# Two pairs of an attention round in one exp over four PSUM banks, the third in an exp of its own, and the vector work of the block moved to VectorE in parts behind the rounds

## What is computed

```
h = layernorm(x) * (1 + ca) + sa
q = h per head times Wq                      # 16 heads of 16 features
scores = q q^T * 4 ; attn = softmax(scores)  # 16 heads, 4096 x 4096
x = x + ga * ((attn q) Wp^T + bp)
h = layernorm(x) * (1 + cb) + sb
f = silu((layernorm(h) * gamma + beta) w1 + b1) w2 + b2     # 256 -> 1024 -> 256, weights dequantized from int32
x = x + gb * (h + 0.5 * f)
```

## Time and profile before

| | |
|---|---|
| median of 3 runs | 2073.87 us (2073.63 to 2074.2) |
| profiled execution, its time | 2074.52 us |
| its span in the trace | 2072.7 us |
| PE matmul busy | 1958.2 us, 94% of the span |
| ACT busy | 1966.9 us, 95% |
| DVE busy | 377.8 us, 18% |
| POOL busy | 70.4 us, 3% |

### The profile page before, as it was taken

The page is one execution under the profiler, slowest core; times in us unless marked ns, Lnnn a source line. Parts: engine busy times, 40 slices in busy tenths (PEclk is TensorE's granted clock), DMA queues, the critical chain, the costliest instruction groups (busy, mean ns, idle before and its releaser), DMA issues.

```text
span 2072.7 us, 42098 instructions
## 1 busy us (share of the span) xinstructions
PE 1958.2 (94%) x18325; PEld 533.5 (26%) x18325; DVE 377.8 (18%) x903; ACT 1966.9 (95%) x2174; POOL 70.4 (3%) x35
## 2 busy tenths in 40 slices
PE   5888889999999999999999999999999999999997
PEld 4311112222222222222222222222222222222224
DVE  7310002210031100410022100311004100231004
ACT  3899999999999999999999999999999999999982
POOL 0000000100010000100001000100001000010000
PEclk9999999999999999999999999999999999999998
DMA  5541111211111221111211111111111112111100
GB/s 160 150 124 46 35 50 41 51 51 42 55 38 48 51 50 51 46 45 41 56 46 50 51 43 53 37 49 51 51 51 45 46 41 56 46 41 41 31 12 12
DMA packets 121337, 108.05 MB, mean 52 GB/s; under 512 B 21936, under 2 KB 120112, under 8 KB 120896
## 3 DMA queue, kind: packets, MB, share of 16 engines
q1 hardware_dynamic: 120400, 103.69, 18.8%
q10 hardware_dynamic: 752, 1.67, 0.2%
HBM read 96.49 MB, written 8.65 MB: 51 GB/s over the span
## 4 chain that ended last, share of the span: by engine, by line
ACT 46%; PE 42%; issue 7%; DVE 1%; ACTq 0%; DVEq 0%
ACT attend_probs L744 45%; PE attend_sums L788 21%; PE attend_scores L776 13%; PE attend_out L796 6%; PE attend_scores L796 1%; PE attend_out L802 1%; PE attend_sums L802 1%; ACT attend_half_tanh L729 1%; ACT attend_ffn_in L753 0%; PE attend_scores L802 0%; DVE attend_st L1085 0%; DVE z L1097 0%; DVE attend_rsqrt_work L91 0%; DVE attend_rsqrt_work L93 0%; DVE attend_rs L95 0%
## 5 line engine op out<-in xcount | busy, mean ns | idle before, releaser
L744 ACT ACTIVATE attend_probs<-attend_scores 128x1024 f32<-128x1024 f32 x2048 | 1891.6, 1038 | 18.6 <-PE attend_scores L776 18.6
L788 PE MATMUL attend_sums<-attend_probs,values 128*17 128x512 f32 x8192 | 1011.2, 597 | 0.0
L776 PE MATMUL attend_scores<-asks,keys 64*128 64x512 f16 x4096 | 673.3, 384 | 74.1 <-ACT attend_probs L744 57.4
L776 PEld LDWEIGHTS attend_scores<-asks,keys 64*128 64x128 f16 x4096 | 150.9, 94 | 886.0 <-ACT attend_probs L744 817.2
L788 PEld LDWEIGHTS attend_sums<-attend_probs,values 128*17 128x17 f32 x8192 | 171.3, 96 | 392.4 <-issue 337.3
L796 PE MATMUL attend_out<-w,hidden 128*32 128x256 f32 x1920 | 124.2, 379 | 0.0
L796 PE MATMUL attend_out<-attend_ffn_in,w 128*32 128x512 f32 x896 | 116.6, 592 | 0.0
L927 DVE COPY attend_sums_sb<-attend_sums 128x512 f32<-128x512 f32 x32 | 22.2, 692 | 487.4 <-PE attend_sums L788 487.4
L991 DVE TENSOR_SCALAR attend_half_in<-attend_out,b_col 128x512 f32<-128x512 f32 x56 | 42.0, 751 | 333.4 <-PE attend_out L796 332.4
L796 PEld LDWEIGHTS attend_out<-w,hidden 128*32 128x32 f32 x1920 | 62.0, 110 | 86.3 <-issue 64.2
L1001 DVE TENSOR_TENSOR base<-attend_out,base 128x512 f32<-128x512 f32 x14 | 9.7, 691 | 376.6 <-PE attend_out L796 376.6
(11 more groups left out here) (140 smaller groups left out, 548.2 us busy)
## 6 DMA issues: line engine op xcount, KB each, us to landing
keys<-parts_dram SPq DMA_DIRECT2D x768, 64.0 KB
keys<-parts_dram SPq DMA_DIRECT2D x256, 56.0 KB
asks<-parts_dram SPq DMA_DIRECT2D x192, 64.0 KB
start_x_in<-L_attn_x SPq DMA_DIRECT2D x8, 512.0 KB, 9.5
parts_dram<-start_q_parts SPq DMA_DIRECT2D x16, 256.0 KB, 2.5
attend_x_now<-L_attn_x SPq DMA_DIRECT2D x8, 512.0 KB, 4.3
out<-base SPq DMA_DIRECT2D x16, 256.0 KB, 2.7
asks<-parts_dram SPq DMA_DIRECT2D x64, 56.0 KB
```

Of the source, the lines that this page charges most:

```text
L744: act.activation(probs[n % P_RING], ps_scores[:, 2 * slot:2 * slot + 2, :], ACT.Exp, scale=scale)\
L776: last = pe.matmul(ps_scores[:, 2 * (n % S_RING) + b, :], keys[rows, part % K_RING, hq, col:col + P], asks[rows, group * Q_HEADS + hq, :], ...
L788: last = pe.matmul(ps_sums[32 * hq:32 * hq + E1, :], values[:, j + STEPS * b, (gg % Q_GROUPS) * Q_HEADS + hq, :], probs[n % P_RING][:, b, ...
```

## The change

The rounds of 2 pairs are moved to the end of the group (rounds 20 and 21). On ACT a round is now one exp over the four banks of its first two pairs (128x2048), and, where the round has three, a second exp over the last two banks (128x1024). A tanh stands between the two. `probs` is one tile of 12 slots, and a round takes three of them in turn (`seat`), so that the two pairs lie side by side. `EXPS` holds the number that `exps_done` has reached when the exp of a pair is done; the first two pairs of a round share it. On PE the scores of pair i in a round wait for the exp of pair i of the round before (`pair_in` finds the pair whose banks these are, past rounds of 2). The order of PE within a round is as it was: all its scores, then its units, then its piece.

GpSimd has no work in the second stage any more. Its bias goes to VectorE in round 12 of a chunk's last group (`add_bias`), its three operations on `base` to rounds 14, 16 and 18 of the third group (`base_of`). VectorE's order is now written by rounds too, and the two layernorms are cut into parts in rounds 8 to 20 of the first group (`norms`). `z1` is no longer made there: `modulate` goes from x1 to `hid` in two operations a tile. `TURN_Z2` and `UP` move one slot on (10 and 12).

```diff
-SIZES = [3] * 10 + [2] + [3] * 10 + [2]
+SIZES = [3] * 20 + [2] * 2
...
-TURN_ATT, PROJECT, TURN_Z2, UP, DOWN = 0, 2, 9, 11, 28
+TURN_ATT, PROJECT, TURN_Z2, UP, DOWN = 0, 2, 10, 12, 28
...
+def exp_order():
+
+    exps, done = {}, 0
+    for gg in range(GROUPS):
+        for r in range(ROUNDS):
+            n = gg * PAIRS + STARTS[r]
+            done += 1
+            exps[n] = exps[n + 1] = done
+            if SIZES[r] == 3:
+                done += 1
+                exps[n + 2] = done
+    return exps
...
+def pair_in(gg, r, i):
+
+    if r < 0:
+        gg, r = gg - 1, r + ROUNDS
+    if gg < 0:
+        return None
+    return gg * PAIRS + STARTS[r] + i if i < SIZES[r] else pair_in(gg, r - 1, i)
...
                 for gg in range(GROUPS):
                     c, group = divmod(gg, Q_GROUPS)
-                    for p in range(PAIRS):
-                        n = gg * PAIRS + p
-                        act.wait_ge(scores_ready, n + 1)
-                        if n % Q_HEADS == 0 and n >= P_RING:
-                            act.wait_ge(steps_done, (n - P_RING) // Q_HEADS + 1)
-                        slot = n % S_RING
-                        act.activation(probs[n % P_RING], ps_scores[:, 2 * slot:2 * slot + 2, :], ACT.Exp, scale=scale)\
-                           .then_inc(exps_done, 1)
-                        if c > 0 and (group, p) in tanh_after:
-                            tanh(c - 1, tanh_after[group, p])
+                    for r in range(ROUNDS):
+                        n = gg * PAIRS + STARTS[r]
+                        act.wait_ge(scores_ready, n + 2)
+                        place_free(act, gg, r, 1)
+                        act.activation(place(gg, r, 0, 2), ps_scores[:, 0:4, :], ACT.Exp, scale=scale).then_inc(exps_done, 1)
+                        if c > 0 and (group, r) in tanh_in:
+                            tanh(c - 1, tanh_in[group, r])
+                        if SIZES[r] == 3:
+                            act.wait_ge(scores_ready, n + 3)
+                            place_free(act, gg, r, 2)
+                            act.activation(place(gg, r, 2), ps_scores[:, 4:6, :], ACT.Exp, scale=scale).then_inc(exps_done, 1)
...
-                    wait(pe, exps_done, n - S_RING + 1)
+                    gone = pair_in(gg, r - 1, i)
+                    if gone is not None:
+                        pe.wait_ge(exps_done, EXPS[gone])
...
                     for r in range(len(SIZES)):
-                        for p in range(STARTS[r], ENDS[r]):
-                            scores(gg, p)
+                        for i in range(SIZES[r]):
+                            scores(gg, r, i)
...
+                        if (group, r) == (3, 12):
+                            add_bias(c)
```

More of the change, by code:

```diff
@@ L53, with seat @@
 SLOTS = len(PLACE_ROUND)
-TURN_ATT, PROJECT, TURN_Z2, UP, DOWN = 0, 2, 9, 11, 28
+TURN_ATT, PROJECT, TURN_Z2, UP, DOWN = 0, 2, 10, 12, 28
+ROUNDS = len(SIZES)
+P_ROUNDS = P_RING // S_RING
+def exp_order():
[9 more added lines that the diff above has]
+    return exps
+EXPS = exp_order()
+def pair_in(gg, r, i):
[4 more added lines that the diff above has]
+    return gg * PAIRS + STARTS[r] + i if i < SIZES[r] else pair_in(gg, r - 1, i)
+def seat(gg, r, i):
+    at, gone = ROUNDS * gg + r, None
+    for back in range(at - P_ROUNDS, -1, -P_ROUNDS):
+        g, q = divmod(back, ROUNDS)
+        if i < SIZES[q]:
+            gone = g * PAIRS + STARTS[q] + i
+            break
+    return S_RING * (at % P_ROUNDS) + i, gone
 class Scope:
@@ L76, in wait, with rsqrt_guess @@
         eng.wait_ge(semaphore, value)
-def rsqrt(dve, y, v, work, step, n):
-    shifted, square = work[:, 0, :], work[:, 1, :]
-    v_eps = work[:, 2, :]
+def rsqrt_guess(dve, y, v, work, step, n):
+    shifted, v_eps = work[:, 0, :], work[:, 2, :]
     k = n * RSQRT_STEPS
@@ L88, in rsqrt, with rsqrt_steps @@
     dve.tensor_scalar(y.bitcast(I32), shifted.bitcast(I32), -1.0, float(0x5F3759DF), ALU.mult, ALU.add).then_inc(step, 1)
-    for i in range(3):
+def rsqrt_steps(dve, y, work, step, n, steps):
+    square, v_eps = work[:, 1, :], work[:, 2, :]
+    k = n * RSQRT_STEPS
+    for i in steps:
         dve.wait_ge(step, k + (3 + 3 * i))
@@ L95, in rsqrt @@
         dve.scalar_tensor_tensor(out=y, in0=square, scalar=1.5, in1=y, op0=ALU.add, op1=ALU.mult).then_inc(step, 1)
-    dve.wait_ge(step, k + RSQRT_STEPS)
+def rsqrt(dve, y, v, work, step, n):
+    rsqrt_guess(dve, y, v, work, step, n)
+    rsqrt_steps(dve, y, work, step, n, range(3))
+    dve.wait_ge(step, (n + 1) * RSQRT_STEPS)
 def adaln_layer(nc, x, wq_t, wp_t, bp, gamma, beta, fc1_q, fc1_s, fc1_b, fc2_q, fc2_s, fc2_b,
@@ L613, in adaln_layer @@
         a = Scope(ctx, nc, "attend")
-        probs = [a.take(f"probs{i}", 2 * BANK).rearrange("p (b n) -> p b n", b=2) for i in range(P_RING)]
+        probs = a.take("probs", P_RING * 2 * BANK).rearrange("p (s n) -> p s n", n=BANK)
         def tok(name):
@@ L647, in wide, with place, place_free @@
             return v.unsqueeze(1).broadcast_to([P, GT, D])
+        def place(gg, r, i, pairs=1):
+            first = 2 * seat(gg, r, i)[0]
+            return probs[:, first:first + 2 * pairs, :]
+        def place_free(eng, gg, r, i):
+            gone = seat(gg, r, i)[1]
+            if gone is not None:
+                eng.wait_ge(steps_done, gone // Q_HEADS + 1)
         def load_x(eng, o):
@@ L772, in scores @@
                         pe.wait_ge(q_in[group], FILL_Q + (FILL_Q + FILL_SHIFT) * c)
-                    wait(pe, exps_done, n - S_RING + 1)
+                    gone = pair_in(gg, r - 1, i)
+                    if gone is not None:
+                        pe.wait_ge(exps_done, EXPS[gone])
                     for b in range(2):
                         rows, col = slice(64 * b, 64 * b + 64), (j % K_STEPS) * P
-                        last = pe.matmul(ps_scores[:, 2 * (n % S_RING) + b, :], keys[rows, part % K_RING, hq, col:col + P],
+                        last = pe.matmul(ps_scores[:, 2 * i + b, :], keys[rows, part % K_RING, hq, col:col + P],
                                          asks[rows, group * Q_HEADS + hq, :], start=True, stop=True)
@@ new lines, in modulate @@
+                def modulate(o, half):
+                    tiles = range(2 * half, 2 * half + 2)
+                    dve.wait_ge(n_rstd, (2 * o + 1) * RSQRT_STEPS)
+                    wait(dve, base_step, 3 * o)
+                    for t in tiles:
+                        last = dve.scalar_tensor_tensor(out=hid[:, t, :], in0=x1[:, t, :], scalar=mo2[:, 0, t, 0:1], in1=mod[:, 2, :],
+                                                        op0=ALU.subtract, op1=ALU.mult)
+                    last.then_inc(scaled, 1)
+                    dve.wait_ge(scaled, 2 * o + half + 1)
+                    for t in tiles:
+                        last = dve.scalar_tensor_tensor(out=hid[:, t, :], in0=hid[:, t, :], scalar=rs2[:, 0, t:t + 1], in1=mod[:, 1, :],
+                                                        op0=ALU.mult, op1=ALU.add)
+                    last.then_inc(hid_ready, 1)
```

141 lines of the change are left out of this document (80 added, 61 removed).

## The result

The changed kernel takes 2153.57 us (median of 4 runs, 2152.05 to 2155.22) against 2074.03 us for the one before, measured beside it. The ratio is 1.0383, with a 95% interval of 1.0365 to 1.0401: 79.5 us slower, where 2155 was forecast.

The account below looks back on a forecast made before the run. ACT was taken to set the pace before, a two-round PE-ACT wait loop after. Chunks 1 to 7 add 68.4 us and chunk 0 adds 12.4, together +81 on 2073.9: 2155 us, range 2131 to 2180.

Parts of the forecast that it names:

- The bound: Three-pair rounds: a wait loop through PE and ACT takes 5.67 us per two rounds, so at least 2.835 us each.
- the five steps: Parts of the two-round loop through PE and ACT: 0.06 + 0.32 + 1.85 + 0.66 + 2.785 = 5.67 us.
- The long exp: ACT's exp over 2048 columns: about 1.88 us, saving 0.067 us of fixed part, bounded by 0.067 more or less.
- Rival 2: The exp over four banks saves nothing, adding 0.067 us in the loop: +26, 2181 us; chance 7%.
- the middle: Assumed long-exp cost, midway between no saving and no fixed part, because rows 7 show equal cost per column.
- The 2-pair rounds: Rounds with two pairs: exp and scores alternate, 2.59 us a round, twice in a group.
- The tanh: On ACT between the two exps, inside the loop: 8 x 0.52 = 4.2 us for each of seven chunks, unabsorbed.
- Costed at nothing: GpSimd's operations moved to VectorE, the cut-up norms and other work hidden beside waits: 0 us, at most 39 uncovered.
- The signs: Expected trace evidence: exp 1.88 us, starts 2.84 apart, ACT idle some 78 us, groups 61.9 or 64.0 us, clock 1.00.
- rival 3: PE's clock falls because PE stops 0.2 us or more each round: +109, 2264 us; chance 3%.
- rival 4: VectorE is late with z2 or a piece, its order fixed by rounds: +35, 2190 us; chance 4%.
- Rival 1: PE's wait is hidden and ACT keeps its pace, loop 5.38 us or less: -12, 2062 us; chance 5%.

Follow-up runs that it names:

- e7: Changed kernel with the short exp cut from 1024 to 768 columns from chunk 1 on: 2093.9 us, ratio 1.0091.
- e4: Changed kernel with PE's third pair of scores behind the round's first unit instead of ahead of it, in three-pair rounds: 2129.1 us, ratio 1.0267.
- e8: Changed kernel with two exps of 1024 columns in the 2-pair rounds, the long exp in three-pair rounds only: 2136.3 us, ratio 1.0300.
- e3: Changed kernel with the tanh behind the short exp instead of between the two exps: 2137.0 us, ratio 1.0306.
- e9: Changed kernel with the piece slots of before (z2 transposes at 9, fc1 from 11), second norm finished in round 18: 2146.7 us, ratio 1.0352.
- e2: Kernel before with only the merged exp and the new order of rounds; GpSimd, VectorE and piece slots as before: 2146.5 us, ratio 1.0351.
- e1: Changed kernel with three exps of 1024 columns a round again, each pair's scores waiting for one exp: 2087.4 us, ratio 1.0067.
- e11: Changed kernel with three exps, old order of rounds, old piece slots and the tanh behind the third exp: 2077.1 us, ratio 1.0016.
- e6: Changed kernel with three exps a round and the 2-pair rounds back in rounds 10 and 21: 2083.4 us, ratio 1.0043.
- e5: Kernel before with only the two 2-pair rounds moved to the end of the group: 2083.6 us, ratio 1.0044.

## Why the prediction was right

**The bound.** "So a three-pair round cannot take less than 2.835 us": 2.83 measured, and each of the five steps came out within 0.01 us of the distance taken from before. e7 shows that it is a loop over two rounds, e4 that its cause is the pair that waits ahead of the units. A chunk took 251.5 us where 251.8 was added up.

**The long exp.** 1.88 us expected, 1.879 measured, between the two bounds. The start of the short exp comes 1.77 us after that of the long one, which leaves 0.067 us for the fixed part that the merge saves. Rival 2 (2181 us) falls by this. The reason given for the middle was thin: rows 7 have two sizes, which give a cost per column but can't show that it holds at 2048, and only the changed kernel does. By the overlap of some 93 ns that the Trainium skill gives (page "ScalarE: Activation LUTs", section "What ACT_TABLE_LOAD costs"), an estimate has that distance some 0.03 us shorter and the total at about 2146 us; the trace's 67 ns stand.

**The 2-pair rounds.** 2.59 us a round was forecast; the long exps there start at 1021.12, 1023.70 and 1026.37 in the changed kernel, 2.58 and 2.67 apart:

```profile
1021.12 1.88 ACT L785 ACTIVATE attend_probs<-attend_scores 128x2048 f32<-128x2048 f32 x1 [0.18 <-PE attend_scores L823]
1023.70 1.88 ACT L785 ACTIVATE attend_probs<-attend_scores 128x2048 f32<-128x2048 f32 x1 [0.70 <-PE attend_scores L823]
1026.37 1.88 ACT L785 ACTIVATE attend_probs<-attend_scores 128x2048 f32<-128x2048 f32 x1 [0.79 <-PE attend_scores L823]
```

e8 undoes them for 17 us.

**The tanh.** "Nothing absorbs it": groups with four tanhs are (63.93 + 63.94)/2 - 61.8 = 2.1 us longer, 4 x 0.53. e3 confirms the place.

**Costed at nothing.** Right for VectorE's and GpSimd's part in the merged kernel (e9 against e2: 0.2 us). Not looked at by itself was the shift of the fc1 slots from 11 to 12: its 7 us (e9) were in the total because the chunk before entered as a measured 242.0 us and the one after was built with all eight tanhs at full price. So the sum was right, and its account was coarser than it read: 14 of the 80 us are not the long exp's (e1). In steps that the runs allow, good to 1 us or so, since the medians of the kernel before differ by that: VectorE's order and the fixed seats +3 (e11), slots and tanh place +6 (e6), order of rounds +4 (e1), the long exp +66 (the changed kernel).

**The signs.** Right: pair 2 starting 0.06 us after the short exp and PE idling 0.21 ahead of it, the groups, the clock at 1.00 (rival 3), no piece waiting for VectorE (rival 4). ACT is idle 101 us for scores, 78 were forecast. Wrong as worded: starts of two long exps "2.84 us apart", which is the average of 2.68 and 2.98, and "ACT idle in front of nearly every long exp". The trace names 326 of 704, since the two loops are shifted and the wait of every second long exp is hidden behind the short exp. The prediction also read the 1270 waits of the earlier trace rows as those of PE's scores; they are of PE's weight loads, and its matmuls waited for exps 127 times, 57.4 us in all, which changes no term. Rival 1, faster, needed a loop of 5.38 us; nothing in the trace gave the missing 0.29.

## What to carry to other kernels

Before merging instructions to save their fixed part, look at what the parts released one by one. Here a ring of three slots freed one by one became two slots freed in lumps, and an engine that waits in order for the last lump holds all that is queued behind it; the 47 us that ACT was to save by the estimate became 66 us lost (e1). Where two engines are both over 90% busy, add up the loop that runs through both of them, over as many rounds as it needs to close, and compare it with each engine's own pace. And look for small jobs that fill an existing gap (here the tanhs, the gaps behind 2-pair rounds): moving the gap cost 9 us (e5), moving the jobs by one slot 7 (e9).

## What the runs showed that I had not expected

**A reordering has its price on PE.** Splitting a round's scores in two cost 0.25 us (e4), since the step from the last scores to the units takes 0.32 us where pair follows pair in 0.22, and the step from a unit back to scores some 0.11 more than from unit to unit.

**GpSimd held VectorE up.** In the kernel before, two of the norms' small operations on 4 columns stretch from 0.17 to over 2 us in each of the seven chunks, while GpSimd prepares `base`. POOL and DVE of the kernel before:

```profile
1089.36 2.40 POOL L717 TENSOR_TENSOR base<-base,b_gb 128x1024 f32<-128x1024 f32 x1
1091.84 2.38 POOL L719 TENSOR_TENSOR base<-base,attend_x 128x1024 f32<-128x1024 f32 x1
...
1089.55 2.24 DVE L88 TENSOR_SCALAR attend_rs<-attend_rsqrt_work 128x4 int32<-128x4 int32 x1
1092.02 2.22 DVE L93 SCALAR_TENSOR_TENSOR attend_rsqrt_work<-attend_rsqrt_work 128x4 f32<-128x4 f32 x1
```

Both VectorE operations end within 0.03 us of the GpSimd operation beside them. The Trainium skill, page "SBUF — State Buffer", section "SBUF: two separate sides", describes a pair of ports that the two engines share under an exclusive lock, which a GpSimd operation holds for its whole length; the trace agrees with that. The page lets a VectorE operation with one SBUF input, as L88 is, be caught only in a mode that uses both ports; whether L88 ran in one no run here shows. In the changed kernel the same operation takes 0.17 us:

```profile
1124.13 0.17 DVE L126 TENSOR_SCALAR attend_rs<-attend_rsqrt_work 128x4 int32<-128x4 int32 x1
```

VectorE's total fell from 377.8 to 375.2 us although it took over four operations a chunk: 1.22 us each there, where GpSimd took 2.4. Part of the fall is that `z1` is no longer made. It was worth no time (e9 against e2, 0.2 us).
